# Head squares on ScalarE, scaling in place in PSUM, Newton steps on GpSimd, and an earlier turn of x, in a two-layer attention and mixture-of-experts kernel

## The reference

```
# layer 1 (cond)
xn  = rms_norm(x, g_norm) * (1 + scale) + shift        # scale, shift = emb @ W_emb + b_emb
q, k, v = xn @ W_qkv                                   # 512 -> 3 x 512
q, k = rms_norm(q, g_q), rms_norm(k, g_k)              # per head of 32
o = softmax(q k^T / sqrt(32)) v
y = o + o @ W_out
# layer 2 (ffn)
h = y + attention(rmsnorm(y))                          # low-rank k, q, v, rotary half, causal
out = x + h + moe(rmsnorm(h))                          # shared expert + 2 of 7 routed experts
```

## Time and profile before

| | us |
|---|---|
| median of 3 runs | 1383.56 |
| lowest and highest | 1382.18, 1387.46 |
| profiled execution, its own time | 1384.72 |
| its span in the trace | 1382.9 |

### The profile page before, as it was taken

One profiled execution on the slowest core, in us unless ns is written; L12 is line 12 of the kernel. 1 busy time (PEld: TensorE's weight loads), 2 busy tenths in 40 slices (PEclk: granted clock), 3 DMA queues, 4 the chain that ended last, 5 costly groups with the idle time before them and its releaser, 6 DMA issues.

```text
span 1382.9 us, 19145 instructions
## 1 busy us (share of the span) xinstructions
PE 1160.5 (84%) x5931; PEld 803.2 (58%) x5931; DVE 861.8 (62%) x1805; ACT 556.3 (40%) x1184; POOL 668.9 (48%) x628
## 2 busy tenths in 40 slices
PE   5978767997799877978988978987878999999980
PEld 5745534653466434634756755755645788888860
DVE  5474696479745894784676685576673675444442
ACT  3333344344434444554445454353353664222220
POOL 1316555565454555665354552442554473555530
PEclk9968978998799878998999988997988999999995
DMA  7063133223322342243437445245343773666669
GB/s 246 23 202 96 38 110 104 71 83 107 107 62 69 116 146 78 78 132 105 130 112 243 113 130 183 77 146 183 109 129 138 267 237 99 108 110 115 112 116 332
DMA packets 90196, 178.45 MB, mean 129 GB/s; under 512 B 13137, under 2 KB 23793, under 8 KB 89073
## 3 DMA queue, kind: packets, MB, share of 16 engines
q1 hardware_dynamic: 81280, 156.90, 35.5%
q0 software_dynamic: 8512, 19.93, 8.0%
q10 hardware_dynamic: 304, 0.40, 0.1%
HBM read 110.86 MB, written 65.27 MB: 127 GB/s over the span
## 4 chain that ended last, share of the span: by engine, by line
PE 59%; DVE 22%; issue 7%; POOL 6%; DMA 3%; ACT 2%; SPq 1%; POOLq 0%; DVEq 0%; ACTq 0%
PE psum L765 8%; PE psum L766 7%; PE psum L767 7%; PE psum L943 5%; PE psum L905 5%; POOL probs L1415 4%; PE psum L1020 3%; PE psum L926 3%; PE psum L1022 3%; PE psum L1021 3%; DVE nmax L1677 3%; PE psum L774 3%; DVE psum L1680 2%; PE psum L1047 2%; PE psum L1049 2%
## 5 line engine op out<-in xcount | busy, mean ns | idle before, releaser
L1415 POOL TENSOR_TENSOR probs<-probs 128x512 f32<-128x512 f32 (+3 forms) x384 | 381.4, 1026 | 173.0 <-PE psum L943 173.0
L1250 ACT ACTIVATE probs<-psum 128x512 f32<-128x512 f32 (+3 forms) x512 | 257.9, 517 | 275.2 <-PE psum L929 138.2
L905 PE MATMUL psum<-stack 96*128 96x512 f32 (+3 forms) x512 | 228.2, 451 | 39.0 <-DVE nmax L1677 18.8
L1677 DVE TENSOR_REDUCE nmax<-psum 128x1 f32<-128x512 f32 x256 | 170.3, 685 | 104.4 <-PE psum L905 100.0
L905 PEld LDWEIGHTS psum<-stack 96*128 96x128 f32 x512 | 105.6, 207 | 191.7 <-issue 133.6
L926 PE MATMUL psum<-stack 97*128 97x512 f32 (+3 forms) x512 | 205.9, 403 | 5.3 <-ACT probs L1250 4.7
L1680 DVE CUSTOM_DVE_ANT_0 psum<-psum,causal 128x128 f32<-128x128 f32 (+3 forms) x256 | 123.0, 504 | 30.2 <-PE psum L905 29.6
L943 PE MATMUL psum<-probs,vals 128*32 128x512 f32 (+3 forms) x1024 | 131.3, 588 | 3.6 <-ACT probs L1250 3.2
L926 PEld LDWEIGHTS psum<-stack 97*128 97x128 f32 x512 | 106.2, 207 | 26.3 <-ACT probs L1250 11.1
L765 PE MATMUL psum<-w_hi,xh 128*128 128x512 f32 (+1 forms) x256 | 101.0, 394 | 23.6 <-POOL xl L1351 19.0
L1457 POOL DMA_INDIRECT acc_s<-tile_y,row_of_slot x38 | 60.5, 1591 | 82.4 <-DVE tile_y L1755 68.8
(11 more groups left out here) (238 smaller groups left out, 2452.8 us busy)
## 6 DMA issues: line engine op xcount, KB each, us to landing
stack<-split_s SPq DMA_DIRECT2D x378, 128.0 KB, 3.1
split_s<-split SPq DMA_DIRECT2D x64, 512.0 KB, 2.8
xt<-in_x_dram SPq DMA_DIRECT2D x4, 1024.0 KB, 5.5
x_s<-yt SPq DMA_DIRECT2D x16, 256.0 KB, 2.5
xt<-x_s SPq DMA_DIRECT2D x4, 1024.0 KB, 5.3
res<-x_s SPq DMA_DIRECT2D x4, 1024.0 KB, 6.3
x_s<-res SPq DMA_DIRECT2D x4, 1024.0 KB, 5.2
tile_rows<-x_s SPq DMA_DIRECT2D x16, 256.0 KB, 5.6
```

Source lines behind the costliest of these rows:

```text
L905: sq.filled(nc.tensor.matmul(psum[:, sq.bank(M), 0:n], st[:, 0, t * P:(t + 1) * P], st[:, 1, 0:n], start=True, stop=True), M)
L1250: sk.cleared(nc.scalar.activation(probs[:, slot, lo:S], psum[:, sk.bank(M), lo:S], ACT.Exp, scale=SCALE), M)
L1415: nc.gpsimd.tensor_tensor(total, total, probs[:, SLOT[step_of(Q, head, t)][0], lo:S], ALU.add).then_inc(s_add, 1)
L1677: sq.cleared(V.tensor_reduce(out, psum[:, sq.bank(M), :], AX.X, ALU.max, negate=True), M)
```

## The change

Five things change, all but the first in layer 1 and in the inverse roots of the later norms.

1. The square of a `qk` product is taken by ACT, straight from the PSUM bank into `vs`, ahead of ACT's copy of the same bank to `qk`. POOL no longer does it. This holds for all four batches of layer 1.
2. For batches 1 to 3, x and q are scaled in place in their PSUM bank by DVE (`value_in_psum`), ACT takes hi from the bank, and DVE takes lo from bank and hi, as separate pieces `x_lo` and `q_lo` one step or so later. `vs` and POOL have no part in it. Batch 0 (and the q of its four groups) stays as it was.
3. For the norms of batches 2 and later and the head norms of batches 1 to 3, DVE only makes the seed (pieces `norm`, `hnorm`), and POOL does the three Newton steps, four instructions each with a wait for its own semaphore after every one (`find_root`, pieces `newton`, `hnewton`). DVE waits for the result at the first `scale` or `hscale`.
4. The table: x of the block after comes at steps 52, 53, 55, 57 (was 60 to 63) in blocks 0 to 2, and for batches 2 and 3 the first two `qk` products of that block come at steps 60 and 62 of the block before it; the rest follow at 1, 3, 5, 9, 15, 21 (was 0, 2, 4, 9, 12, 15, 20, 24). `hnorm` is at 23 (was 27), `scale` at 42 to 47 (was 51 to 54), the last `v` at 47 (was 52).
5. `sum` and `o` stand first in their step, ahead of the other pieces.

```diff
@@ beside_heads
+    put(range(SUM_STEP, 64, STEPS_Q), each("sum", k, NQD - 1))
+    put(range(SUM_STEP + 2, 64, STEPS_Q), each("o", k, NQD - 1))
...
-        for n, m in enumerate((17, 18, 20, 21, 24, 25, 26, 27) if k == 0 else (0, 2, 4, 9, 12, 15, 20, 24)):
+        if k:
+            put((0,), [("hsum", j, 1)])
+        for n, m in enumerate((17, 18, 20, 21, 24, 25, 26, 27) if k == 0 else (1, 3, 5, 9, 15, 21), 0 if k == 0 else 2):
...
-        put((30, 31, 32, 33) if k == 0 else (27, 28, 29, 30), each("hnorm", j, 4))
+        put((29, 30) if k == 0 else (23, 24), [("hnorm", j, 0), ("hnewton", j)])
...
-            put((44, 45, 46, 47), norm)
-            put((51, 52, 53, 54), scale)
+            put((38, 39) if k == 0 else (36, 37), norm)
+            put((45, 46, 47, 48) if k == 0 else (42, 43, 46, 47), scale)
+            if phase(after) == 1:
+                put((53, 54, 56, 58), each("x_lo", after, NC))
+            put((52, 53, 55, 57), each("x", after, NC))
+            if phase(after) == 1:
+                put((60, 62), each("qk", after, 2))
+                put((62,), [("hsum", after, 0)])
...
-            put((26, 27, 28, 30), norm)
+            put((26, 27), norm)
...
@@ scalar, qk
-                        ring.cleared(copy(qk[:, t, c * D:(c + 1) * D], bank_of(key)), key)
+                        if n >= 2:
+                            act.wait_ge(hsum, n - 1)
+                        nc.scalar.activation(vs[:, n % 2, :], bank_of(key), ACT.Square).then_inc(hsq, 1)
+                        ring.cleared(copy(qk[:, t, c * D:(c + 1) * D], psum[:, ring.bank(key), :]), key)
@@ gpsimd
+            def find_root(key, x, y, t):
+
+                pool.wait_ge(seeded, ROOT_NO[key] + 1)
+                for n in range(3):
+                    plink(nc.gpsimd.tensor_tensor(t, y, y, ALU.mult))
+                    plink(nc.gpsimd.tensor_tensor(t, t, x, ALU.mult))
+                    plink(nc.gpsimd.tensor_scalar(t, t, -0.5, 1.5, ALU.mult, ALU.add))
+                    plink(nc.gpsimd.tensor_tensor(y, y, t, ALU.mult))
+                pool.sem_inc(rooted, 1)
@@ vector
+            def value_in_psum(key, s1, s2):
+
+                ring.wait_full(dve, key)
+                bank = psum[:, ring.bank(key), :]
+                if s2 is None:
+                    V.tensor_scalar(bank, bank, s1, None, ALU.mult).then_inc(moved, 1)
+                else:
+                    V.tensor_scalar(bank, bank, s1, s2, ALU.mult, ALU.add).then_inc(moved, 1)
```

89 lines of the change are left out of this document (63 added, 26 removed).

## The result

The changed kernel takes **1370.12 us** (median of 5 runs, 1366.62 to 1375.44) against 1385.42 for the kernel before (5 runs beside it, 1382.18 to 1387.70). The ratio is 0.989, with a 95% interval from 0.986 to 0.992: faster by 1.1%, where 4.7% was forecast. 1370 lies outside the range (1296 to 1364). The direction was right, the size a quarter of the forecast.

A forecast was written before the change was run, and what follows sets the result against it. PE was taken to bound steps 0 to 23, DVE 24 to 51, nobody 52 to 63. Terms -23.2 - 8.9 - 37 + 9 - 0.5 - 3 = -63.6 took 1384.7 to 1321.1 us profiled, 1320 median; range 1296 to 1364.

The forecast's parts named there:

- (a): Starts of blocks 1 to 3: x ready before its products, so gaps and slow products go; -23.2 us in sum.
- (b): Starts of blocks 1 and 2: two products fewer there, 4.5 us off each; -8.9 us, returning in steps 52 to 63.
- (c): Blocks 0 to 2, steps 24 to 51: Newton steps leave DVE, 51 us of its work, of which 37 us is time.
- (d): Blocks 0 to 2, steps 52 to 63: added lo, products and bank waits cost 3.5, 3.5 and 2 us; +9 in sum.
- (e): Head squares on ACT: longer bank hold costs nothing, last start-up square is done sooner; -0.5 us.
- (f): Blocks 3 to 5: Newton steps leave DVE, but POOL's chain precedes the rotary add; -3 us in block 3, nothing elsewhere.
- the 45 that was named as a sign: Sign for the block-start terms: steps 0 to 23 of block 1 come to near 45 us.
- a clock that stays at 0.8 in steps 24 to 63: Sign of being wrong by most: PE's clock stays there, so what DVE gives back goes to slow matmuls.
- the two banks bind: Rival, steps 52 to 60: eight items each wait the whole 2.7 us chain, 21 us a block; no change, 1384; chance 0.07.
- GpSimd's prices: POOL's Newton chain: 0.29 to 0.45 us an instruction plus waits at 128x128, 6 us for heads; 4 us for 128x4.
- from 644 us on, the same lengths: Sign for blocks 3 to 5: from 644 us of the kernel before on, stretches keep their lengths.
- The gap at the start of block 3: The 7.93 us gap waits for POOL's split of layer 2's weights and stays; nothing counted.

The follow-up runs named there:

- e5: Changed kernel with x turned late (steps 60 to 63), all eight products at the block's start, layer 2's Newton steps on DVE: 1346.47 us, ratio 0.972.
- e10: Changed kernel with x still early, but its first two q and k products back at the block's start: 1371.87 us, ratio 0.991.
- e2: Changed kernel with x turned late again (steps 60 to 63) and all eight products at the block's start: 1356.05 us, ratio 0.979.
- e7: Kernel before, its order kept, with only the new forms (scaling in PSUM, lo on DVE, head squares on ACT), Newton on DVE: 1380.87 us, ratio 0.998.
- e8: As e5, but the Newton steps of blocks 0 to 2 also on DVE, at the new places: 1358.65 us, ratio 0.980.
- e11: e8 with only the norm of x back at steps 44 to 47 and its scaling at 51 to 54: 1366.97 us, ratio 0.987.
- e1: Changed kernel with all Newton steps back on DVE, at the steps of the seeds: 1366.14 us, ratio 0.986.
- e6: Changed kernel with the head squares back on GpSimd, from the copied qk: 1369.38 us, ratio 0.989.
- e3: Changed kernel with layer 2's Newton steps (blocks 3 to 5) back on DVE: 1357.39 us, ratio 0.982.
- e15: e5 with two of four x chunks early (1342.1 us), and layer 2's weights split at steps 51 to 60 instead of 57 to 63: 1333.26 us, ratio 0.962.
- e12: Kernel before, all its forms kept, with only its table changed to the places of e8: 1371.63 us, ratio 0.991.
- e4: Changed kernel with lo of x chunks 1 and 2 first in DVE's queue in steps 54 and 56, blocks 0 and 1: 1364.59 us, ratio 0.985.

## Why the prediction was wrong, by its own steps

The forecast's terms belong to stretches of the blocks, and the two profiled executions can be held against it stretch by stretch. The borders are the exponentials of steps 0, 24 and 52, summed over blocks 0 to 2:

| stretch | terms | forecast | measured |
|---|---|---|---|
| steps 0 to 23 | (a), (b) | -32.1 | -21.1 |
| steps 24 to 51 | (c) | -37 | -24.1 |
| steps 52 to 63 | (d) | +9 | +21.0 |
| all else | (e), (f) | -3.5 | +6.1 |
| sum | | -63.6 | -18.1 |

Part of the first and third row is a matter of borders: 2.5 us of each gap of 5.92 lay ahead of the block's start, so its loss shortens steps 52 to 63. That is why steps 0 to 23 of block 1 came to 49.0 us, all but 0.4 of them busy on PE, and not to the 45 that was named as a sign. It makes (d) larger still, some 26 us. Every term missed in the same direction.

**(a), (b) and (d) together: -23.1 forecast, +4 to +11 measured** (the forms' -3.3 and the early x's +14.1 by the ratios, -3.2 and +6.8 from step 24 on, -4.6 and +11.5 in blocks 0 to 2). This is the step that failed. Its parts:

- (a) The gaps themselves went as forecast: 1.82 us ahead of batch 1's first product where a chain of 2.1 was worked out, none ahead of batch 2's.

```profile
115.42 0.47 PE L781 MATMUL psum<-w_hi,xh 128*128 128x512 f32 x1 [1.82 <-DVE xl L1560]
```

What was wrong is the credit. The sum booked 8.2 us for each of two block starts, and took the early place for what brings them. But with x late and lo on DVE the gap is already down to 1.84 us and the product behind it at 0.40 to 0.47 us an instruction (e5). The early place had only that rest to win.
- (b) Right in sign and emptied by its own sentence "they return in (d)": e10 shows -2.6 on one side and +2.8 on the other.
- (d) The mechanism was written down to the item (lo of chunk 1 behind `sum` and `hscale`, the turn of k behind `o`, the row maxima behind lo of chunk 3), and these are the very waits of the trace. They were priced at 3.5 us for a block. In block 1 they are 9.8 us of PE where before had 3.8, and the stretch is 34.4 us, not 29 to 30; block 0 has 33.7 where 23.9 was, block 2, without products, 26.8 where 23.6 was. Two things were left out of the price. One is shown: with these waits PE's matmuls took longer, at a lower granted clock (0.65 in e10, 0.84 and 0.71 in e2), which is 4.2 of 7.4 us in block 1 and 2.0 of 7.1 in block 0. The forecast had named a clock that stays at 0.8 in steps 24 to 63 as a sign of being wrong. In block 1 it was 0.87 in steps 24 to 51 and 0.70 in 52 to 63. The other is our reading, not shown by itself: each wait stands in a loop, where a late bank makes the turn late, and so ACT's hi and DVE's scaling behind it. The rival "the two banks bind" had the whole chain, 2.7 us with eight items, 21 us for a block, which is more than twice what came. Its mechanism was the one at work, and its size was as wrong as the forecast's.

**(c): -37 forecast, -25 to -35 for places and engine together** (e7 to e5). The size is not far off, by luck, since the reason was wrong. The forecast put all of it down to leaving DVE. Some 20 us came with the new places (e7 to e8, where products, sums and v move too; the norm of x alone is worth 8 to 12 of them, e11), and the engine alone brought 6 by the landmarks of blocks 0 to 2, 11 by the ratios. In block 1 DVE's work in steps 24 to 51 fell to 39.3 us, near the 37 worked out, and the stretch lost 7.5 us where 14 were counted. The earlier trace rows held the clue: the same instruction at 0.29 and 1.26 us, by what GpSimd did beside it. The text used this to price the seeds, and not to ask what the Newton steps would cost at the seeds' steps on DVE. e1 answers: 19.6 us in all, of which a third to a half is on the path. And in the changed kernel this gain hides behind the banks: stage 40 to 56 stands at 34.6 with early x, at 27.9 without.

**GpSimd's prices** were right: 0.40, 0.46, 0.30, 0.46 us at 128x128, 5.7 us for the chain (6 forecast); 0.20 us at 128x4, 3.3 to 3.6 for the chain (4 forecast). In blocks 1 and 2 DVE doesn't wait for it. In block 0 it waits 1.00 us at `hscale`, and the chain pushes GpSimd's sums on, so that `sum` on PE waits 4.69, a wait that e1 does not have:

```profile
170.45 1.94 PE L874 MATMUL psum<-probs,ones_for_sums 128*32 128x512 f32 x8 [4.69 <-POOL probs L1456]
```

The forecast named these sums ahead of the chain and not those behind it. On GpSimd the Newton steps cost some 7 us in layer 2 and bring some 6 in blocks 0 to 2 by the landmarks, 10 and 11 by the ratios. The Trainium skill has a rule on this (GPSIMD Engine Reference, Engine selection): elementwise work on a tile belongs on VectorE. This case agrees in layer 2 and not in blocks 0 to 2, by these numbers.

**(e): -0.5 forecast, nothing measured** (e6).

**(f): -3 forecast, some +7 measured** (+6.5 from before to after, +6.7 between the medians of the kernels with and without; +9 to +11 by e3 alone). The text said that the chain stands ahead of the rotary add for which the turn at 32 waits, and then counted a gain. The turn's wait grew from 0.74 us to 3.88, 3.44 and 3.81 in the three blocks, nearly the chain's 3.5, and part of it is made good in block 4 (step 40 to 56: 20.4 us before, 17.0 after). No gain from DVE's relief shows. The sign "from 644 us on, the same lengths" failed too: blocks 4 and 5 lost 4.5 and 4.0 us between steps 24 and 40, where no change was forecast.

**The gap at the start of block 3** stayed, 8.37 us where 7.93 was, as forecast, and for the reason given (e15).

By terms, the miss of 50 us is 27 to 34 from (a), (b) and (d), 2 to 12 from (c), about 10 from (f). The range was too narrow at the upper end since it let only (c) and a doubled (d) fail. It left (f) without a bound and counted (a) as certain.

## What to carry to other kernels

- Before an instruction is moved to another engine, ask what it would cost on its own engine at another place. Where its length varies fourfold with what a neighbour does (0.29 and 1.26 us here), the place is the cheaper remedy: e12 got with a table alone what the whole change got.
- A buffer that several kinds of work pass in turn has a capacity. Before more is sent through it in one stretch, list what each release waits for, and price the loop and the clock that PE falls to in it, not the single wait. Two of four chunks early, with their lo first in the queue, gained 4 us; all four lost 7 to 14.
- A chain on an engine that is idle on average can cost nearly its full length where its queue leads to the critical path. Look at what stands behind it, not only at its consumer.

## What the runs showed of the hardware

**The same code at two clocks.** Up to step 24 of block 0 the changed kernel, e4, e5 and e8 issue the same instructions in the same order (e6 differs in the engine of the squares). The stretch from the first exponential to the first `o_hi` took 44.1, 48.3, 44.1 and 49.8 us in them, and 43.6 in e6. The table of windows, columns as in the earlier trace rows, shows 113 to 133 us of the changed kernel (first fence) and of e4 (second):

```profile
113.00:133.00 20.00, 17.99 (x79) 13.03 (x80) 8.85 (x15) 9.34 (x19) 5.23 (x5) 1.00 0.37 101
```

```profile
113.00:133.00 20.00, 18.80 (x72) 12.90 (x71) 7.37 (x12) 7.88 (x15) 4.90 (x4) 0.80 0.32 91
```

The granted clock was 1.00 (2.4 GHz throughout) in one and 0.80, a mixture of 1.2 and 2.4 GHz, in the other. In the 24 us ahead (89 to 113 us) PE had been busy 19.6 us in both, and the clock there was 0.89 and 0.78. e5 and e8, with 44.1 and 49.8 us, ran on the same chip. So the level granted to the same work is not the same in every execution. That alone is 4 us of a run, as much as several of the edits here, and it is why stages were compared beside medians. What decides it stays open.

**How long a small DVE instruction in SBUF takes** follows what GpSimd does beside it over a factor of five to nine: 128x4 at 0.16 us where GpSimd stands idle (e8, 311.8 to 327.6 us, with the nine instructions of the norm between 315.3 and 321.9), 0.85 to 0.97 us on average at steps 44 to 47 (e11), 1.42 in the dearest group of the kernel before. For a scaling of 128x512 the two were 477 ns (e11, at 51 to 54) and 1153 ns (e8, at 42 to 48).
